# All three taps of w placed behind W's first mix and V's second level in VectorE's order

## The chip, the cores and the metric

The kernel runs on one core of a Trainium2 chip. The metric is the device time of one execution in microseconds (us), here the median of several runs. The five engines are TensorE (PE in the rows; PEld is its weight load), VectorE (DVE), ScalarE (ACT), GpSimd (POOL) and SyncE (SP). Each works through a queue of its own in order, and they wait for each other by semaphores.

## The reference, cut to what matters

A layer of gated slot attention over 4 sequences of 512 tokens with 16 heads of width 128, then a small feed-forward layer. Per head and sequence, h being the hidden states:

```python
q, k = short_conv(h @ Wq, cq), short_conv(h @ Wk, ck)
v, w = short_conv(h @ Wv, cv), short_conv(h @ Ww, cv)
g, beta = log_sigmoid(h @ Wf1 @ Wf2), sigmoid(h @ Wb)
w = l2norm(w)
# for each token t, with gt = exp(g_t) and bw = beta_t * w_t
Sk = Sk * gt + outer(k_t, bw)
Sv = Sv * gt + outer(bw, v_t)
a = softmax(q_t @ Sk * SCALE)
o_t = a @ Sv
```

short_conv is a causal filter of four taps over time for each channel, followed by silu. Its last tap (the present token) is a scaling; the other three are multiply-adds with the projection shifted by 1, 2 and 3 tokens. These three are "the taps" below.

## The kernel before

The recurrence over time is cut into levels of blocks of doubling length. 64 units (16 heads by 4 sequences) go through a pipeline: a slot is one pass of the loop over `slots(H, B)`, and in slot n unit n (`u1`) is projected and filtered, unit n-1 (`u2`) makes its scores level by level, unit n-2 (`u3`) takes them back level by level and makes the outputs, unit n-3 (`u4`) is normed and projected out, and unit n-4 (`u5`) is added up in memory. There are 68 slots; slots 2 to 63 hold all of u1, u2 and u3.

Every engine has its own copy of that loop, written out by hand. Nothing plans it: what stands earlier in an engine's body runs earlier, and each operation waits for the semaphores that it names.

What touches the change:

- `project(u, i)` on TensorE (lines 722 and 726 and on): six products into `proj_ps`, for w (i = 0), q (1), k (2), v (3). w and q use the same bank, `CONV_BANK = (0, 0, 1, 1)`.
- `tap` on ScalarE (line 347) scales the projection into `conv`. `conv_tap(dve, u, i, k)` on VectorE (line 591) adds the tap k = 0, 1, 2. The first waits for ScalarE's `tap_done`, the second and third for `conv_step` of the tap before. Each reads `proj_ps`.
- `tanh` on ScalarE (line 356) waits for the third tap. `silu_w` on VectorE (line 602) multiplies tanh and filter.
- On TensorE, `project(u1, 1)` for q stands at r = 1 of the slot and waits for `conv_step` of w's third tap, because it writes the bank that the taps read. Behind it come the projection of f (line 397) and the rest of the slot.
- `level_scores(pe, u2, r)` on TensorE (line 755 for r = 0 and 1, 777 from r = 2) makes the r-th level of V in `V_ps`, from the coarsest down. `descend(dve, u2, r)` on VectorE scales V between two levels: line 676 clears a part at r = 0, line 681 is r = 1, line 687 from r = 2. Each waits for the level before on TensorE, and the next level there waits for it.
- `mix_products(pe, u3, lev)` (line 806) and `mix_ends` (line 813) on TensorE, `mixable` (710) and `mix` (715, a masked copy) on VectorE and `grow_W` (298) on GpSimd take the scores back, from level 0 up. The masked copy of level 0 is "W's first mix". The third mix product on TensorE (level 2) is the first that waits for it, and stands behind `level_scores` of r = 1.

TensorE's order around the place is: `mix_ends`, mix product of level 1, key-query product, turn of U, `level_scores` r = 0, turn of U, `level_scores` r = 1, mix product of level 2, `project(u1, 1)`.

Of the kernel before, what the change touches and what calls it, by code (L numbers as in the profile page):

```python
# [61 lines left out]
def build(nc, x, Wq, Wk, Wv, Ww, cq, ck, cv, Wf1, Wf2, Wb, Wg1, Wg2, bg2, norm_w, Wo,  # L62
# [14 lines left out]
    with ExitStack() as ctx:  # L77
# [254 lines left out]
        def filt(u, i, k):  # L332

            return coefs[:, COEF_OF[i], u.h, k:k + 1]
# [251 lines left out]
        def conv_tap(dve, u, i, k):  # L586

            back = k + 1
            dve.wait_ge(tap_done, u.count(4, i + 1)) if k == 0 else dve.wait_ge(conv_step, u.count(12, 3 * i + k))
            y_ = conv[:, CONV_BUF[i], back:T]  # L590
            nc.vector.scalar_tensor_tensor(y_, proj_ps[:, CONV_BANK[i], 0:T - back], filt(u, i, KW - 1 - back), y_,  # L591
                                           ALU.mult, ALU.add).then_inc(conv_step, 1)
# [78 lines left out]
        def descend(dve, u2, r):  # L671

            lev = LEVELS - 1 - r
            if r == 0:
                wait(dve, V_done, u2.count(1, 0))
                nc.vector.memset(V_ps[:, 0:P], 0.0).then_inc(V_step, 1)
                return
            dve.wait_ge(V_ps_ready, u2.count(9, r))
            if r == 1:
                v = V_ps[:, 3 * P - 1:T]  # L680
                nc.vector.tensor_scalar(v, v, chunk_tot(u2.par, 2), None, ALU.mult).then_inc(V_step, 1)
                return
            if r == 2:
                v = V_ps[:, T - 1:T]
                nc.vector.tensor_scalar(v, v, chunk_tot(u2.par, 3), None, ALU.mult).then_inc(V_step, 1)
            v = after_odd(V_ps[:, :], lev)
            nc.vector.tensor_tensor(v, v, block_tot(u2.par, lev, 0), ALU.mult).then_inc(V_step, 1)  # L687
# [612 lines left out]
        def _(dve):  # L1300
# [7 lines left out]
            for s in slots(H, B):  # L1308
                u1, u2, u3, u4 = s.u1, s.u2, s.u3, s.u4
# [7 lines left out]
                if u2:  # L1317
# [1 line left out]
                    conv_tap(dve, u2, 3, 1)  # L1319
                    conv_tap(dve, u2, 3, 2)  # L1320
                    descend(dve, u2, 0)
                if u1:
                    conv_tap(dve, u1, 0, 0)
                    conv_tap(dve, u1, 0, 1)
                if u3:
                    mixable(dve, u3, 0)
                    mix(dve, 0)
# [2 lines left out]
                if u2:  # L1330
                    descend(dve, u2, 1)
                if u1:
                    conv_tap(dve, u1, 0, 2)
                for r in range(1, LEVELS):
                    if u2 and r > 1:
# [339 lines left out]
```

## Time and profile before

| | |
|---|---|
| median of 3 runs | 1989.41 us |
| lowest, highest | 1987.39, 1990.56 us |
| the profiled execution | 1987.3 us |
| its span, first to last instruction | 1985.6 us |
| granted TensorE clock, mean | 0.987 of full speed |
| busy: TensorE, VectorE | 97%, 89% of the span |
| busy: ScalarE, GpSimd | 70%, 67% |

The profile is of one execution. A busy time counts overlapping instructions once. Matmuls are pipelined and their ends are modelled, so their busy share is an upper look. The idle time of an engine before an instruction is shown in brackets with what ended it; idle times that are hidden under the end of the instruction ahead are not shown. A group of instructions in a timeline runs from the first start to the last end.

### The profile page before, as it was taken

To read this page: it belongs to the slowest core of one execution; us is meant where nothing else is said; L and a number is where in the kernel's file an instruction comes from. 1 tells how busy PE (TensorE), PEld (TensorE's weight loads), DVE (VectorE), ACT (ScalarE), POOL (GpSimd) and SP (SyncE) were. 2 spreads that over 40 slices of the span, in tenths; PEclk is the share of its full clock that TensorE was granted. 3 is DMA by queue.
4 is the path that set the end of the run, shared out by engine and by line. 5 is a ranking of instruction groups with operands and counts; after the bars stand their busy time and mean duration, and the time that the engine had idled before them with its cause. 6 is when DMAs were issued, how large, how long until landed. Compare 5 with 4: busy or idle time off the path is not lost.

```text
span 1985.6 us, 41492 instructions
## 1 busy us (share of the span) xinstructions
PE 1921.0 (97%) x12192; PEld 1623.8 (82%) x12192; DVE 1774.2 (89%) x4096; ACT 1395.3 (70%) x3986; POOL 1333.7 (67%) x2289
## 2 busy tenths in 40 slices
PE   7999999999999999999999999999999999999897
PEld 5778888888888888888888888888888888887776
DVE  5699999999999999999999999999999999998587
ACT  4467777777777777777777777777777777777543
POOL 5376676777677676767677676767677676766444
PEclk8899999999999999999999999999999999999899
DMA  3021111111111111111111110111111110112300
GB/s 78 1 61 21 27 34 24 26 24 33 26 24 27 27 34 20 30 24 33 27 24 26 27 35 15 36 24 33 23 27 26 24 37 14 25 22 43 63 22 33
DMA packets 53645, 58.51 MB, mean 29 GB/s; under 512 B 14896, under 2 KB 44720, under 8 KB 53424
## 3 DMA queue, kind: packets, MB, share of 16 engines
q0 software_dynamic: 9216, 33.56, 11.5%
q1 hardware_dynamic: 44208, 22.29, 4.1%
q8 instruction: 104, 1.70, 0.3%
q14 instruction: 117, 0.96, 0.2%
HBM read 20.19 MB, written 37.75 MB: 29 GB/s over the span
## 4 chain that ended last, share of the span: by engine, by line
PE 85%; POOL 7%; DVE 4%; issue 2%; ACT 1%; DMA 0%; POOLq 0%; DVEq 0%; ACTq 0%
PE proj_ps L722 15%; PE mix_ps L806 11%; PE V_ps L777 10%; PE work_ps L931 8%; PE work_ps L937 7%; PE tr_ps L746 6%; PE V_ps L755 5%; PE work_ps L1608 5%; PE proj_ps L397 4%; PE work_ps L826 3%; PE mix_ps L813 2%; POOL w_lo L370 2%; PE tr_ps L786 2%; PE work_ps L828 2%; PE proj_ps L1479 1%
## 5 line engine op out<-in xcount | busy, mean ns | idle before, releaser
L591 DVE SCALAR_TENSOR_TENSOR conv<-proj_ps,coefs,conv 128x511 f32<-128x511 f32 (+2 forms) x768 | 561.2, 731 | 9.9 <-ACT conv L347 3.0
L298 POOL TENSOR_TENSOR W<-W,tot 128x256 f32<-128x256 f32 x384 | 256.0, 667 | 245.3 <-PE mix_ps L806 245.1
L1059 POOL TENSOR_TENSOR A_lev<-A,masks 128x256 f32<-128x256 f32 x448 | 319.2, 717 | 0.1
L806 PE MATMUL mix_ps<-W,U 128*128 128x128 f32 x1792 | 294.6, 286 | 9.8 <-POOL W L298 4.3
L777 PE MATMUL V_ps<-A_lev,UT 128*128 128x128 f32 x1792 | 286.6, 283 | 1.4 <-DVE V_ps L687 1.4
L806 PEld LDWEIGHTS mix_ps<-W,U 128*128 128x128 f32 x1792 | 256.2, 192 | 35.7 <-issue 20.2
L715 DVE COPY_PREDICATED A<-masks,mix_ps 128x256 f32<-128x256 uint32 x448 | 268.5, 599 | 6.6 <-PE mix_ps L806 6.5
L584 DVE TENSOR_TENSOR wT<-wT,tot 128x128 f32<-128x128 f32 x768 | 233.2, 343 | 40.3 <-DVE U L567 1.8
L777 PEld LDWEIGHTS V_ps<-A_lev,UT 128*128 128x128 f32 x1792 | 238.0, 193 | 23.2 <-DVE V_ps L687 23.0
L356 ACT ACTIVATE th<-conv 128x512 f32<-128x512 f32 x256 | 162.3, 634 | 104.3 <-DVE conv L591 103.3
L722 PE MATMUL proj_ps<-hT_hi,w_hi 128*128 128x512 f32 x512 | 222.2, 434 | 4.2 <-DVE conv L591 2.4
L567 DVE COPY U<-wT 128x256 f32<-128x256 f32 x448 | 204.5, 457 | 7.2
L429 ACT ACTIVATE UT<-tr_ps 128x512 f32<-128x512 f32 (+1 forms) x256 | 139.1, 543 | 100.2 <-PE tr_ps L746 99.3
L687 DVE TENSOR_TENSOR V_ps<-V_ps,tot 128x256 f32<-128x256 f32 x384 | 163.8, 427 | 50.3 <-PE V_ps L777 50.2
L722 PE MATMUL proj_ps<-hT_hi,w_lo 128*128 128x512 f32 x512 | 203.0, 396 | 0.0
L722 PE MATMUL proj_ps<-hT_lo,w_hi 128*128 128x512 f32 x512 | 202.1, 395 | 0.0
L931 PE MATMUL work_ps<-qk 128*128 128x512 f32 (+3 forms) x512 | 182.2, 458 | 3.7 <-POOL qk L622 2.7
L298 POOL TENSOR_TENSOR W<-W,gT 128x256 f32<-128x256 f32 x64 | 54.2, 846 | 194.0 <-PE mix_ps L806 194.0
L347 ACT ACTIVATE conv<-proj_ps,coefs 128x512 f32<-128x512 f32 x256 | 175.4, 685 | 8.5 <-PE proj_ps L722 8.5
L414 ACT ACTIVATE A<-work_ps,fac 128x512 f32<-128x512 f32 (+3 forms) x256 | 128.0, 529 | 62.9 <-PE work_ps L931 62.6
L660 ACT ACTIVATE y_sb<-work_ps,rms 128x256 f32<-128x256 f32 x256 | 107.3, 471 | 55.0 <-PE work_ps L1608 54.9
L746 PE MATMUL tr_ps<-ident,U 128*128 128x128 f32 x896 | 140.1, 273 | 0.0
(204 smaller groups left out, 4763.2 us busy)
## 6 DMA issues: line engine op xcount, KB each, us to landing
head_sum<-y_sb POOLq DMA_DIRECT2D x64, 512.0 KB, 6.5
w_raw<-in_L_attn_Ww SPq DMA_DIRECT2D x16, 128.0 KB, 2.2
w_raw<-in_L_attn_Wq SPq DMA_DIRECT2D x16, 128.0 KB, 2.2
w_raw<-in_L_attn_Wk SPq DMA_DIRECT2D x16, 128.0 KB, 2.3
w_raw<-in_L_attn_Wv SPq DMA_DIRECT2D x16, 128.0 KB, 2.2
wo_raw<-in_L_attn_Wo SPq DMA_DIRECT2D x16, 128.0 KB, 2.0
head_sum<-in_L_attn_hidden_states SPq DMA_DIRECT2D x1, 2048.0 KB, 10.0
acc<-head_sum SPq DMA_DIRECT2D x4, 512.0 KB, 3.8
```

The lines of the kernel that those rows point to most:

```text
L298: nc.gpsimd.tensor_tensor(w, w, block_tot(u3.par, lev, 0), ALU.mult).then_inc(W_step, 1)
L347: nc.scalar.activation(conv[:, CONV_BUF[i], :], proj_ps[:, CONV_BANK[i], :], ACT.Copy, scale=filt(u, i, KW - 1)).then_inc(tap_done, 1)
L567: nc.vector.tensor_copy(Ulev(u, lev).rearrange("p (n e l) -> p n e l", e=2, l=L), merged(X, lev))\
L584: nc.vector.tensor_tensor(x_, x_, odd_tot(u.par, lev, e), ALU.mult).then_inc(U_step, 1)
L591: nc.vector.scalar_tensor_tensor(y_, proj_ps[:, CONV_BANK[i], 0:T - back], filt(u, i, KW - 1 - back), y_, ALU.mult, ALU.add).then_inc(conv ...
L715: nc.vector.copy_predicated(dst, mask_cols(lev).bitcast(U32), mix_cols(lev % 2, lev)).then_inc(mix_done, 1)
L722: last = nc.tensor.matmul(dst, w[:, k, :], x_(k), start=(k == 0 and n == 0), stop=(k == KT - 1 and n == 2))
L746: last = nc.tensor.transpose(tr_ps[:, n * P:(n + 1) * P], block_, ident[:, :])
L777: last = nc.tensor.matmul(dst, UT[:, i % 2, at:at + P], A_lev[:, lev, 2 * p:2 * p + 2, :], start=False, stop=True, skip_group_check=True)
L806: last = nc.tensor.matmul(mix_ps[:, half, p * P:(p + 1) * P], Ulev(u3, lev)[:, p * P:(p + 1) * P], after_odd(W[:, p * T // 2:(p + 1) * T / ...
L931: nc.tensor.matmul(work_ps[:, A_BANK[c], c * P:T], qk[:, 1, c * P:(c + 1) * P], qk[:, 0, c * P:T], start=True, stop=True).then_inc(A_ps_re ...
L1059: nc.gpsimd.tensor_tensor(dst, diag_after_odd(lev), mask_cols(lev), ALU.mult)\
```

## The change

VectorE's order at the beginning of a slot is changed, and nothing else. Before: v's three taps and the clearing of V (`descend` 0), w's first and second tap, W's first mix, V's second level (`descend` 1), w's third tap. After: v's three taps and the clearing, W's first mix, `descend` 1, all three taps of w. The instructions and what each of them waits for are the same.

```diff
@@ -1319,9 +1319,6 @@
                     conv_tap(dve, u2, 3, 1)
                     conv_tap(dve, u2, 3, 2)
                     descend(dve, u2, 0)
-                if u1:
-                    conv_tap(dve, u1, 0, 0)
-                    conv_tap(dve, u1, 0, 1)
                 if u3:
                     mixable(dve, u3, 0)
                     mix(dve, 0)
@@ -1330,6 +1327,8 @@
                 if u2:
                     descend(dve, u2, 1)
                 if u1:
+                    conv_tap(dve, u1, 0, 0)
+                    conv_tap(dve, u1, 0, 1)
                     conv_tap(dve, u1, 0, 2)
                 for r in range(1, LEVELS):
                     if u2 and r > 1:
```

## Rows read from the trace of the kernel before

**Rows 1.** The page: busy us, share of the span and instructions of each engine.

```profile
PE 1921.0 (97%) x12192; PEld 1623.8 (82%) x12192; DVE 1774.2 (89%) x4096; ACT 1395.3 (70%) x3986; POOL 1333.7 (67%) x2289
```

**Rows 2.** The page: the chain that ended last, by engine.

```profile
PE 85%; POOL 7%; DVE 4%; issue 2%; ACT 1%; DMA 0%; POOLq 0%; DVEq 0%; ACTq 0%
```

**Rows 3.** Window of four slots: length, busy PE, PEld, DVE, ACT, POOL, PEclk, DMA share, GB/s.

```profile
1018.00:1130.00 112.00, 110.82 (x717) 93.76 (x716) 103.93 (x241) 83.32 (x243) 78.94 (x139) 1.00 0.16 27
```

**Rows 4.** The chain in order of time, slot 35: start us, us, what.

```profile
1017.60 0.44 PE tr_ps L746 x4
...
1018.06 0.71 PE V_ps L755 x4
1018.77 0.53 PE mix_ps L806 x4
1019.30 1.39 PE proj_ps L722 x6
```

**Rows 5.** Timeline of VectorE, slot 35: start, us, engine, line, what, forms, count [idle].

```profile
1013.08 2.31 DVE L591 SCALAR_TENSOR_TENSOR conv<-proj_ps,coefs,conv 128x511 f32<-128x511 f32 x3
...
1015.49 1.46 DVE L591 SCALAR_TENSOR_TENSOR conv<-proj_ps,coefs,conv 128x511 f32<-128x511 f32 x2
...
1016.93 0.72 DVE L715 COPY_PREDICATED A<-masks,mix_ps 128x256 f32<-128x256 uint32 x1
1017.64 0.36 DVE L681 TENSOR_SCALAR V_ps<-V_ps,tot 128x129 f32<-128x129 f32 x1
1017.91 0.74 DVE L591 SCALAR_TENSOR_TENSOR conv<-proj_ps,coefs,conv 128x509 f32<-128x509 f32 x1
1018.57 0.75 DVE L611 SCALAR_TENSOR_TENSOR vT<-th,conv 128x256 f32<-128x256 f32 x2
```

**Rows 6.** Timeline of VectorE, slot 35, the second tap of w alone.

```profile
1016.20 0.75 DVE L591 SCALAR_TENSOR_TENSOR conv<-proj_ps,coefs,conv 128x510 f32<-128x510 f32 x1
```

**Rows 7.** Timeline of TensorE's weight loads, slot 35.

```profile
1018.05 0.52 PEld L755 LDWEIGHTS V_ps<-A,UT_top 128*128 128x128 f32 x4 [0.25 <-DVE V_ps L681]
...
1019.01 0.19 PEld L722 LDWEIGHTS proj_ps<-hT_hi,w_hi 128*128 128x128 f32 x1
```

**Rows 8.** Timelines of VectorE and TensorE at the place, slots 2, 7 and 63.

```profile
91.82 0.36 DVE L681 TENSOR_SCALAR V_ps<-V_ps,tot 128x129 f32<-128x129 f32 x1 [0.22 <-PE V_ps L755]
92.09 0.74 DVE L591 SCALAR_TENSOR_TENSOR conv<-proj_ps,coefs,conv 128x509 f32<-128x509 f32 x1
...
93.22 0.50 PE L722 MATMUL proj_ps<-hT_hi,w_hi 128*128 128x512 f32 x1
...
231.15 1.03 PE L755 MATMUL V_ps<-A,UT_top 128*128 128x257 f32 x4
...
232.40 0.39 DVE L681 TENSOR_SCALAR V_ps<-V_ps,tot 128x129 f32<-128x129 f32 x1
...
1803.34 0.74 DVE L591 SCALAR_TENSOR_TENSOR conv<-proj_ps,coefs,conv 128x509 f32<-128x509 f32 x1
...
1804.47 0.50 PE L722 MATMUL proj_ps<-hT_hi,w_hi 128*128 128x512 f32 x1
```

**Rows 9.** Timeline of ScalarE, slot 35: the tanh of w.

```profile
1018.74 0.63 ACT L356 ACTIVATE th<-conv 128x512 f32<-128x512 f32 x1 [1.48 <-DVE conv L591]
```

**Rows 10.** Timeline of VectorE, slot 35: V's next two steps behind the place.

```profile
1022.10 0.43 DVE L687 TENSOR_TENSOR V_ps<-V_ps,tot 128x256 f32<-128x256 f32 x1 [0.21 <-PE V_ps L777]
...
1023.89 0.43 DVE L687 TENSOR_TENSOR V_ps<-V_ps,tot 128x256 f32<-128x256 f32 x1 [0.20 <-PE V_ps L777]
```

**Rows 11.** Line 397 (ns min/median/max), a wait of TensorE, and two windows as in rows 3.

```profile
L397 PE MATMUL proj_ps<-f_hi,wf_hi x64: 393/394/628, 20.6 to 1806.0; 128*128 128x512 f32 x64
...
1836.59 0.57 PE L806 MATMUL mix_ps<-W,U 128*128 128x128 f32 x3 [1.25 <-POOL W L298]
...
1845.00:1850.00 5.00, 2.55 (x16) 1.54 (x14) 3.60 (x15) 3.27 (x11) 1.01 (x1) 0.96 0.02 5
1850.00:1855.00 5.00, 3.85 (x17) 3.49 (x16) 1.16 (x3) 4.90 (x11) 2.02 (x3) 0.50 0.21 15
```

## The prediction

> **What bounds the kernel now.** I read the busy shares first. TensorE is busy for 1921.0 of 1985.6 us, VectorE for 1774.2 [rows 1], and in a steady stretch of four slots TensorE records 110.82 of 112 us, VectorE 103.93 [rows 3]. The chain that ended last says the same by another way: 85% of it is TensorE's [rows 2]. So a slot is TensorE's queue in its order, and it comes round every 28.05 us: from 92.09 in slot 2 to 1803.34 in slot 63 for the same tap, over 61 slots [rows 8]. Recorded idle of TensorE is (112 - 110.82) / 4 = 0.30 us a slot, and that is all the slack that a wait could eat.
>
> Then I read one slot (slot 35) at the place of the change. In the chain in order of time, the first level's products of V end at 1017.60, TensorE turns U until 1018.04, V's second level runs from 1018.06 to 1018.77, a mix product to 1019.30, and from there the projection of q [rows 4]. On VectorE's side the second level's step of V (line 681) starts at 1017.64, 0.04 us behind the product that it waits for [rows 4, 5]. It has that same 0.04 us in 61 of 64 slots; slot 2 shows the wait with its name, 0.22 us on V_ps [rows 8]. Only slots 1, 7 and 56 have VectorE itself arriving last (slot 7: the product ends at 231.15 + 1.03 = 232.18, the step starts at 232.40 [rows 8]). So **VectorE meets TensorE at line 681 and is a little early there already**.
>
> The third tap of w follows it: start 1017.91, 0.74 us, end 1018.65 [rows 5]. TensorE's projection of q writes the bank that w's taps read, so it waits for that third tap. Its weight load starts at 1019.01, 0.36 us behind the tap's end [rows 7]. Between V's step and the projection the delay is fixed: in all 62 slots from 2 to 63 the projection's first product starts 1.13 us behind that tap's start (92.09 to 93.22, 1803.34 to 1804.47 [rows 8]).
>
> **The change part by part.**
>
> *Two taps leave the place ahead of the first mix.* They took 1.46 us there (from 1015.49) [rows 5]. The copy and the masked copy of the first mix come up to 1.4 us earlier; the far ends of the mix products, for which they wait, are ready at about the time at which the taps started. Who gains? V's step at line 681 doesn't: it waits for the product that ends at 1017.60, and nothing ahead of that product waits for a tap. The next user of the mix on TensorE stands behind V's second level in its own order, at 1018.77 [rows 4], over a microsecond behind the masked copy's end at 1017.65 [rows 5]. So this part is worth 0, and VectorE gets about 1.3 us more of idle time ahead of line 681 instead. The cover is that TensorE is last at line 681; in the three slots where it isn't, the gain is at most 0.2 to 0.5 us once, under 1 us in the run.
>
> *The two taps come in behind line 681.* All three now run in one chain, each waiting for the one before. The price of such a chain stands in the same slot: v's three taps take 2.31 us from start to end [rows 5]. Beginning 0.27 us behind V's step (1017.64 to 1017.91), they end 2.58 us behind it, where the one tap ended at 1.01. That is 1.57 us later. The other bound goes by w's own first two: the second starts at 1016.20, 0.71 us behind the first [rows 6], and not (2.31 - 0.74) / 2 = 0.79; with it for the first step the chain ends at 0.27 + 0.71 + 0.79 + 0.74 = 2.51, that is 1.50 us later.
>
> *TensorE waits for the third.* It had 0.36 us between the tap's end and the weight load. Of that a signal from VectorE needs some 0.05 us: V's step ends at 1018.00, the load that it releases starts at 1018.05 [rows 5, 7]. Slack is thus 0.31 us, and the stall is 1.50 - 0.31 = 1.19 to 1.57 - 0.31 = 1.26 us a slot. I take the middle, **1.22 us**. The projection of q and all behind it in TensorE's queue (f's projection, the levels of V, the turns, the mix products) move by that. Below nothing it can't go, since no instruction of TensorE between line 681 and the projection gets shorter.
>
> The Trainium skill, page "VectorE: DVE Perf Modes", section "The DRAIN you can't avoid", says that between VectorE operations a semaphore after each costs nothing over the flush that takes place anyway. The rows disagree: an operation that doesn't wait for the tap ahead starts 0.66 us behind its start (1017.91 to 1018.57 [rows 5]), a tap that waits 0.71 to 0.79 us. What the page's rule would give is the third rival below.
>
> *Who else is behind the taps?* VectorE's silu of v and V's next steps come 1.5 us later, 0.3 more than TensorE does. They were early: the masked copy after them let VectorE wait 0.21 and 0.20 us at V's next two steps [rows 10], which takes up 0.3 and brings VectorE back to TensorE's pace. On ScalarE the tanh of w waits for the third tap: it had waited 1.48 us [rows 9], and now waits 1.5 longer. The evacuation of U behind it moves by the same 1.5, and its reader on TensorE stands behind both projections, which take 1.39 us for q's six products alone [rows 4]. GpSimd has no operation that waits for a tap of w here, and no DMA or queue of SP is moved.
>
> **The sum.** Slots 2 to 63, 62 of them, pay 1.22 us: 75.6 us. Slot 0 has no V and no mix, so the order is the same; in slot 1 setup products lie between the tap and the projection and cover it; slot 64 and on have no w. The profiled execution took 1987.3 us (span 1985.6 and 1.7 around it), so it becomes 2062.9. The median of the runs shown lies 2.1 us above that execution, which gives 2065.0. I give **2064**, between both. In the profile I expect a slot of 29.27 us.
>
> **The rivals.**
>
> *Part of the stall is given back.* Waits of TensorE later in the slot for something that isn't late would shrink. All its recorded idle is 0.30 us a slot [rows 3], so at least 1.19 - 0.30 = 0.89 us a slot is left, and with it 55 us: 2043. Half of it gives 2054. Against it: most of these waits end on VectorE's or ScalarE's answer to a product of TensorE itself, and they move along.
>
> *VectorE's lag is not made up.* If it is the bound behind the taps, its whole 1.57 us goes round in each slot: 62 x 1.57 = 97 us, 2085. For it speaks its load (93% in the stretch [rows 3]), against it the two waits in [rows 10].
>
> *A cheaper chain.* If waiting taps followed each other like operations that don't wait, at 0.66 us, the third would end at 0.27 + 0.66 + 0.66 + 0.74 = 2.33 us behind V's step, 1.32 us later than now, and the stall would be 1.32 - 0.31 = 1.01 us: 63 us, 2051. The taps in [rows 5, 6] that already wait speak against it. (By the Trainium skill's section named above it would come out so.)
>
> *Clock.* Now TensorE would stand for over a microsecond in every slot. In this trace it stood 1.25 us until 1836.59, and the clock was still 0.96 from 1845 to 1850; it was 0.50 from 1850 to 1855, after a stretch in which TensorE was busy for only 2.55 of 5 us [rows 11]. Were each stall followed by the lower level (1.2 GHz) for the nine products of the two projections, each would take 0.63 in place of 0.39 us [rows 11]: 9 x 0.23 = 2.1 us a slot, 130 us more, 2194. [...] No steady slot of before shows a gap that long, so this is left to the run; I give it little, since 1.25 us did nothing.
>
> *Faster.* VectorE is the one that is late at line 681, as in slot 7. Then the step moves forward by all of that lateness, and V's second level with it. It decides from a lateness of 1.2 us, where it outweighs the stall; at the full 1.46 us of the two taps the gain is 0.24 us a slot, 15 us: 1972. The trace has 0.5 us at the most, in one slot.
>
> *It does nothing.* The projection would have to be released by something later than the taps. Then the time stays at 1989. The weight load follows so closely that 1.2 us more of cover isn't there.
>
> **How the numbers follow.** Chances: forecast (1.10 to 1.32 us a slot, 2057 to 2071) 0.60; part given back (2043 to 2057) 0.12; cheaper chain (about 2051) 0.03; VectorE's lag (2071 to 2085) 0.14; clock 0.04; more given back than recorded idle, 1995 to 2043, 0.03; no change 0.02; faster 0.02. A measurement of this kernel can tell about 0.2% from no change. The range takes in the first four and a few us beyond for the unknown costs: 2040 to 2087. Faster 0.02, same 0.02, slower 0.96.
>
> **What would show it.** Right: in VectorE's timeline the masked copy ends over a microsecond ahead of line 681 and a wait on V_ps stands before that; the three taps follow as one group of about 2.3 us; the weight load of the projection of q shows an idle time of about 1.2 us, released by the tap (line 591); the slot is 29.2 to 29.3 us. Wrong: line 681 moving forward against the end of the product before it; idle time of TensorE in the rest of the slot that shrinks (part given back) or grows at V's levels (VectorE's lag); a granted clock below 1.00 between 120 and 1850 us.

## The result

The changed kernel took 2067.86 us (median, 2067.6 to 2068.94), the kernel before 1989.99 us beside it: a ratio of 1.0394, 95% interval 1.0379 to 1.0408. That is 77.9 us slower; 2064 was forecast, from a sum of 75.6 us.

The page of the changed kernel, in the parts that answer to [rows 1, 2]: busy times and the chain that ended last by engine.

```profile
span 2067.2 us, 41492 instructions
...
PE 1941.5 (94%) x12192; PEld 1627.9 (79%) x12192; DVE 1777.6 (86%) x4096; ACT 1396.8 (68%) x3986; POOL 1326.4 (64%) x2289
...
PE 79%; DVE 10%; POOL 7%; issue 2%; ACT 1%; DMA 0%; POOLq 0%; DVEq 0%; ACTq 0%
```

VectorE's busy time is the same to 3.4 us, so it does no more work. Its share of the chain went from 4% to 10%: in each slot the chain now leaves TensorE for VectorE. The place shows in the chain in order of time, slot 35 of the changed kernel (start us, us, what), which answers to [rows 4].

```profile
1060.62 0.88 PE V_ps L755 x4
1061.51 0.02 issue
1061.53 0.36 DVE V_ps L681
1061.89 0.66 DVE conv L591
1062.55 0.02 issue
1062.58 0.76 DVE conv L591
1063.34 0.02 issue
1063.36 0.76 DVE conv L591
1064.12 0.04 issue
1064.16 1.65 PE proj_ps L722 x6
```

From the end of V's first level the chain runs through V's step and the three taps to the projection of q. Before, TensorE's own products filled that stretch. The timelines of VectorE and of TensorE's weight loads in the same slot answer to [rows 5, 7].

```profile
1059.31 0.17 DVE L676 MEMSET V_ps<- 128x128 f32 x1
1059.65 0.17 DVE L710 COPY A<-mix_ps 128x4 f32<-128x4 f32 x1 [0.18 <-PE mix_ps L813]
1059.73 0.73 DVE L715 COPY_PREDICATED A<-masks,mix_ps 128x256 f32<-128x256 uint32 x1
1061.53 0.36 DVE L681 TENSOR_SCALAR V_ps<-V_ps,tot 128x129 f32<-128x129 f32 x1 [1.08 <-PE V_ps L755]
1061.80 2.30 DVE L591 SCALAR_TENSOR_TENSOR conv<-proj_ps,coefs,conv 128x511 f32<-128x511 f32 x3
1064.02 1.25 DVE L611 SCALAR_TENSOR_TENSOR vT<-th,conv 128x256 f32<-128x256 f32 x2
```

```profile
1061.94 0.52 PEld L755 LDWEIGHTS V_ps<-A,UT_top 128*128 128x128 f32 x4 [0.25 <-DVE V_ps L681]
1062.39 0.57 PEld L806 LDWEIGHTS mix_ps<-W,U 128*128 128x128 f32 x4
1064.16 0.19 PEld L722 LDWEIGHTS proj_ps<-hT_hi,w_hi 128*128 128x128 f32 x1 [1.20 <-DVE conv L591]
```

The mix is over at 1060.46, and VectorE then idles 1.08 us until V's first level ends. The weight load of the projection starts 1064.16 - 1061.53 = 2.63 us behind line 681, where it was 1019.01 - 1017.64 = 1.37 [rows 5, 7]: **1.26 us later**, the upper of the two bounds. The slot is 29.30 us, from 94.77 in slot 2 to 1882.03 in slot 63 for the first tap behind line 681, over 61 slots; before it was 28.05 [rows 8].

### The profile page after: what moved, and what is told of

Same layout as the page of the kernel before. It is cut to its first block, busy times and chain, and to the rows that moved or that the text cites. A ratio compares the mean times of both kernels' runs of the same rounds, so it can differ in the third digit from the quotient of the medians.

```text
span 2067.2 us, 41492 instructions
## 1 busy us (share of the span) xinstructions
PE 1941.5 (94%) x12192; PEld 1627.9 (79%) x12192; DVE 1777.6 (86%) x4096; ACT 1396.8 (68%) x3986; POOL 1326.4 (64%) x2289
## 4 chain that ended last, share of the span: by engine, by line
PE 79%; DVE 10%; POOL 7%; issue 2%; ACT 1%; DMA 0%; POOLq 0%; DVEq 0%; ACTq 0%
PE proj_ps L722 16%; PE mix_ps L806 10%; PE V_ps L777 9%; PE work_ps L931 8%; DVE conv L591 7%; PE work_ps L937 7%; PE tr_ps L746 5%; PE work_ps L1607 5%; PE proj_ps L397 4%; PE V_ps L755 3%; PE work_ps L826 3%; PE mix_ps L813 2%; POOL w_lo L370 2%; PE tr_ps L786 2%; PE work_ps L828 2%
## 5 line engine op out<-in xcount | busy, mean ns | idle before, releaser
L591 DVE SCALAR_TENSOR_TENSOR conv<-proj_ps,coefs,conv 128x511 f32<-128x511 f32 (+2 forms) x768 | 566.8, 738 | 12.4 <-ACT conv L347 3.2
L1059 POOL TENSOR_TENSOR A_lev<-A,masks 128x256 f32<-128x256 f32 x448 | 309.1, 695 | 0.1
L777 PEld LDWEIGHTS V_ps<-A_lev,UT 128*128 128x128 f32 x1792 | 237.9, 192 | 23.5 <-DVE V_ps L687 23.3
L722 PEld LDWEIGHTS proj_ps<-hT_hi,w_hi 128*128 128x128 f32 x512 | 97.1, 190 | 103.5 <-DVE conv L591 76.9
```

Source lines behind the costliest of these rows:

```text
L722: last = nc.tensor.matmul(dst, w[:, k, :], x_(k), start=(k == 0 and n == 0), stop=(k == KT - 1 and n == 2))
L777: last = nc.tensor.matmul(dst, UT[:, i % 2, at:at + P], A_lev[:, lev, 2 * p:2 * p + 2, :], start=False, stop=True, skip_group_check=True)
L1059: nc.gpsimd.tensor_tensor(dst, diag_after_odd(lev), mask_cols(lev), ALU.mult)\
```

## The experiments

The theory: TensorE stands because w's third tap ends later behind line 681, and passing the mix is free. Rivals: the order against the mix costs (A); VectorE is the bound and its idle time is what is paid (B); the waits in themselves cost, whatever their length (C); a tap ahead of the mix is always free (D).

### Past the mix alone

```diff
                 if u1:
-                    conv_tap(dve, u1, 0, 0)
-                    conv_tap(dve, u1, 0, 1)
                 if u3:
                     mixable(dve, u3, 0)
                     mix(dve, 0)
+                if u1:
+                    conv_tap(dve, u1, 0, 0)
+                    conv_tap(dve, u1, 0, 1)
```

> The kernel before, with w's first two taps moved behind the first mix but still ahead of V's step at line 681; the third stays behind it. Theory (TensorE stalls for the taps that stand between line 681 and the projection of q; passing the mix is worth nothing): the third tap still ends about 1.0 us behind line 681, no stall. VectorE may wait some 0.18 us for the far ends ahead of the copy and reach line 681 that much later: 1990 to 2002 us, no stall of 1.2 us at the projection. Rival A (it is the order against the mix that costs): near 2068. Rival B (VectorE is the bound, and the 1.08 us that it idles ahead of line 681 in the changed kernel is what is paid): that idle time is filled again, so near 1990 too; this run doesn't tell B from the theory.

Measured: 1999.29 against 1990.27 us, ratio 1.0045 (1.0028 to 1.0062), 9 us. Its timeline of VectorE, slot 35:

```profile
1021.85 0.17 DVE L710 COPY A<-mix_ps 128x4 f32<-128x4 f32 x1 [0.17 <-PE mix_ps L813]
1021.93 0.73 DVE L715 COPY_PREDICATED A<-masks,mix_ps 128x256 f32<-128x256 uint32 x1
1022.45 1.50 DVE L591 SCALAR_TENSOR_TENSOR conv<-proj_ps,coefs,conv 128x511 f32<-128x511 f32 x2
1023.87 0.35 DVE L681 TENSOR_SCALAR V_ps<-V_ps,tot 128x129 f32<-128x129 f32 x1
```

Rival A is out. What the move past the mix costs is one idle time of 0.17 us ahead of the copy, whose far ends aren't ready so early; no wait stands before line 681 any more, so VectorE is last there. TensorE's weight load behind that line (1024.28) shows 0.38 us of idle time, where it had 0.25 [rows 7], and 9 us over 62 slots is 0.15 us each. Nearly all of the 78 us belongs to passing line 681.

### One tap moved

```diff
-                    conv_tap(dve, u1, 0, 1)
...
+                    conv_tap(dve, u1, 0, 1)
                     conv_tap(dve, u1, 0, 2)
```

> The kernel before, with only the second tap of w moved behind line 681 (one ahead of the mix, two in a chain behind). Theory: the third tap ends 0.27 + 0.78 + 0.75 = 1.80 us behind line 681, 0.79 later than before, less 0.31 of slack: a stall of 0.48 us in 62 slots, 30 us, 2020. Without any slack it would be 0.79 x 62 = 49 us, 2039; if half of the whole price is paid, 2029. Rival B (VectorE's idle time ahead of line 681 is what costs): about 0.4 to 0.5 us of idle time a slot, the same 25 to 31 us.

Measured: 2017.79 us, 27.5 us more than before (ratio 1.0140, 1.0124 to 1.0155). TensorE's weight load:

```profile
1034.62 0.19 PEld L722 LDWEIGHTS proj_ps<-hT_hi,w_hi 128*128 128x128 f32 x1 [0.42 <-DVE conv L591]
```

It starts 1.84 us behind line 681 (1032.78), 0.47 later than before; times 62 that is 29 us. One tap costs 28 us and two cost 78, not 56: the first pays only beyond the slack of 0.31 us, the second pays in full (1.26 - 0.47 = 0.79 us at the load, 49 us; the medians are 50 us apart). That is a threshold, as the sum had it, and not a price for each tap.

### The two taps cut short, at either place

```diff
-            y_ = conv[:, CONV_BUF[i], back:T]
-            nc.vector.scalar_tensor_tensor(y_, proj_ps[:, CONV_BANK[i], 0:T - back],
+            w_ = 8 if i == 0 and k < 2 and 1 < u.off else T - back
+            y_ = conv[:, CONV_BUF[i], back:back + w_]
+            nc.vector.scalar_tensor_tensor(y_, proj_ps[:, CONV_BANK[i], 0:w_],
```

> The kernel before with w's first two taps cut to 8 columns in slots 2 to 63 (part of the filter is left out; every wait and signal stays). VectorE loses about 1.2 us of work a slot ahead of the first mix. Theory (TensorE is last at line 681; what stands ahead of the mix is free): no gain beyond some 3 us, 1986 to 1991. Rival B (VectorE, busy 93% of a steady stretch, is the bound): its 1.2 us comes back in each slot, 74 us, 1916.

> The changed kernel with the same two taps cut to 8 columns (part of the filter is left out). Theory: the price is the length of the chain behind line 681; two short taps of 0.2 to 0.25 us with their waits bring the third tap's end to 1.4 to 1.6 us behind line 681, 0.4 to 0.6 later than before, less 0.31 of slack: 0.1 to 0.3 us a slot, 1996 to 2009. Rival C (the place and the waits in themselves cost, not the length): above 2040.

Measured: in the kernel before 1989.9 against 1990.51 us (ratio 0.9997, 0.9987 to 1.0007); in the changed kernel 2002.25 us (ratio to the kernel before 1.0057, 1.0042 to 1.0072). VectorE with the short taps in the kernel before, slot 35:

```profile
1019.38 0.42 DVE L592 SCALAR_TENSOR_TENSOR conv<-proj_ps,coefs,conv 128x8 f32<-128x8 f32 x2
1019.75 0.17 DVE L711 COPY A<-mix_ps 128x4 f32<-128x4 f32 x1
1019.83 0.72 DVE L716 COPY_PREDICATED A<-masks,mix_ps 128x256 f32<-128x256 uint32 x1
1021.53 0.36 DVE L682 TENSOR_SCALAR V_ps<-V_ps,tot 128x129 f32<-128x129 f32 x1 [0.98 <-PE V_ps L756]
```

The 1.46 us of [rows 5] became 0.42 us, and the 1.04 us of work that is gone turned into 0.98 us of idle time ahead of the step of V. Nothing came out at the end: rival B is out for this place in the kernel before. In the changed kernel the same cut gives back 66 of 78 us: the three taps take 1.26 us there in place of 2.30. So the length of the chain is what is paid, and rival C is out.

### The stall filled on TensorE

```diff
-        PROJ_AT = (1, 2, 4, 5)
+        PROJ_AT = (1, 3, 4, 5)
...
-                        pe.wait_ge(conv_step, u1.count(12, 3))
-                        pe.wait_ge(low_done, 4 * u1.h + 2)
-                        project(u1, 1)
                         pe.wait_ge(wf_low, u1.h + 1)
...
                         three_products(proj_ps[:, 1, :], wf_hi, wf_lo, ...)
+                        pe.wait_ge(conv_step, u1.count(12, 3))
+                        pe.wait_ge(low_done, 4 * u1.h + 2)
+                        project(u1, 1)
```

`PROJ_AT` tells ScalarE which of the projections of a unit it waits for; q's is the third now.

> The changed kernel, with TensorE's projection of f (the other bank, no wait for w's taps) moved ahead of the projection of q. VectorE's order and work are those of the changed kernel. Theory: f's three products (0.70 us) run inside the stall, q starts at the same 2.6 us behind line 681, the stall shrinks from 1.26 to 0.56 us: 62 x 0.70 = 43 us back, 2025. Rival B (VectorE is the bound): filling TensorE's wait gives nothing, 2060 to 2068. If the tap of q on ScalarE, 0.7 us later against the rest, becomes a new wait: between.

> The kernel before with the same exchange of f and q on TensorE, as the control of the run above. Theory: there is no stall to fill, q comes 0.7 us later and its readers have room: 1990, within 6. If q's lateness costs, it shows here: up to 0.7 x 62 = 43 us more, 2033.

Measured: 2042.3 us for the changed kernel with f first, 1992.11 us for the control (ratio 1.0011, 1.0002 to 1.0021). VectorE's order was left as it was and 25.6 us came back, which rules B out for the changed kernel too; but it isn't 43. What is missing stands in the waits of that run (waiting engine, tile and line, released by: us in total, times, longest), the second of which the kernel before and the changed one have once, for 0.4 us:

```profile
PEld proj_ps L722 <- DVE conv L591: 46.7, 63, 2.6
...
PEld V_ps L755 <- DVE V_ps L687: 25.9, 63, 0.6
```

With f no longer behind q, V's third level follows q's products at once, and meets V's step (line 687), which stands on VectorE behind the three taps and the silu of v. To test that, the silu of v was moved behind that step:

```diff
                     if u2 and r > 1:
                         descend(dve, u2, r)
-                    if u2 and r == 1:
-                        silu_v(dve, u2)
+                    if u2 and r == 2:
+                        silu_v(dve, u2)
```

> The changed kernel with f ahead of q on TensorE (2042 us) and, on VectorE, the silu of v moved behind V's next step. In the run without this move only 26 of the 43 us expected came back, and a new wait stood at V's third level (line 755, released by line 687, 25.9 us in 63 times). Theory: that wait is VectorE's lag behind the taps, laid open because f's products no longer cover it; without silu of v (1.25 us) ahead of that step it goes: 0.28 x 62 = 17 us back, 2025. If the lag isn't the cause, 2042. If v's turn on TensorE becomes late instead, between.

Measured: 2027.2 us (ratio to before 1.0178, 1.0159 to 1.0197), 15 us less, and the wait at line 755 on line 687 is down to 0.4 us, once. So VectorE's lag at that step of V is real, but in the changed kernel it lies under the projection of f.

### All three taps ahead

```diff
                     conv_tap(dve, u1, 0, 1)
+                    conv_tap(dve, u1, 0, 2)
...
-                if u1:
-                    conv_tap(dve, u1, 0, 2)
```

> The kernel before with all three taps of w ahead of the first mix, so none behind line 681. Theory: the copy and the masked copy come 0.75 us later, line 681 has 0.19 us in hand (it could start 0.52 us behind the masked copy's start and starts 0.71 behind), so V's second level and all of TensorE behind it move by about 0.55 us, while the wait for the tap at the projection is gone: 62 x 0.55 = 34 us, 2024. Rival D (a tap ahead of the mix is always free): 1990.

Measured: 2031.41 us (ratio 1.0201, 1.0186 to 1.0217), 41 us more; 34 were expected. The weight loads, slot 35:

```profile
1040.54 0.52 PEld L755 LDWEIGHTS V_ps<-A,UT_top 128*128 128x128 f32 x4 [0.91 <-DVE V_ps L681]
1040.98 0.57 PEld L806 LDWEIGHTS mix_ps<-W,U 128*128 128x128 f32 x4
1041.49 0.19 PEld L722 LDWEIGHTS proj_ps<-hT_hi,w_hi 128*128 128x128 f32 x1
```

Now the wait is V's: 0.91 us where it was 0.25 [rows 7], and none before the projection. 0.66 us times 62 is 41 us, so the 0.55 us expected were 0.11 too few. Rival D is out. Of the places tried for the three taps, the kernel before has the cheapest: two fit ahead of line 681, one behind it.

### The same kind of move where the step of V looks late

In the kernel before, TensorE waits 0.39 us for V's step of r = 7, and on VectorE k's first tap stands ahead of that step.

```diff
-                    if u1 and r in (6, 7):
-                        conv_tap(dve, u1, 2, r - 6)
+                    if u1 and r == 7:
+                        conv_tap(dve, u1, 2, 0)
+                        conv_tap(dve, u1, 2, 1)
```

> The kernel before with the same kind of move at another place, where the step of V may be what is late: the first tap of k goes behind V's step of r = 7 (line 687), for which TensorE's weight load waits 0.39 us. The reader of that chain of taps (the last tap of k, then tanh and the projection of v in the next slot) has over 2 us. Theory: V's step comes some 0.65 us earlier, TensorE's products before it end only 0.02 us before the level starts, so at most 0.1 to 0.15 us a slot comes back: 6 to 9 us, 1982. If the recorded 0.39 us were all real, 24 us, 1966. If the later taps of k are read sooner than that, slower: 2000.

Measured: 2024.97 us, 33 us more (ratio 1.0168, 1.0154 to 1.0182). The waits before and in this run at line 826, the outputs; the profile names no releaser there:

```profile
PEld work_ps L826 <- issue: 18.0, 62, 0.3
```

```profile
PEld work_ps L826 <- issue: 62.5, 63, 1.2
```

A miss of mine. The outputs wait for the masked copy of level 6, and both taps stand ahead of that copy, as they did before. What is new stands in VectorE's timeline of the run, slot 35:

```profile
1053.98 0.43 DVE L687 TENSOR_TENSOR V_ps<-V_ps,tot 128x256 f32<-128x256 f32 x1 [0.23 <-PE V_ps L777]
1054.33 0.48 DVE L715 COPY_PREDICATED A<-masks,mix_ps 128x256 f32<-128x256 uint32 x1
1054.68 1.51 DVE L591 SCALAR_TENSOR_TENSOR conv<-proj_ps,coefs,conv 128x511 f32<-128x511 f32 x2
```

The first tap used to run in the time ahead of V's step, where VectorE now waits 0.23 us, and the two taps now wait for each other. The copy ended at 1056.56, and the outputs' weights loaded from 1056.73. The gain at V's level was had, and more was lost one wait further on.

The run beside it had in addition the low part of k's weights behind the silu of k on GpSimd, in the slots ahead of a new head.

```diff
                     low_weights(pool, s.next_h, 1)
-                    low_weights(pool, s.next_h, 2)
...
                     silu_qk(pool, u1, 2)
+                if s.next_h:
+                    low_weights(pool, s.next_h, 2)
```

> The kernel of the run with k's tap behind V's step, and on GpSimd, in the slots ahead of a new head, the low part of k's weights (0.75 us) behind the silu of k instead of ahead of it. In these slots (one in four, 28.35 us against 27.86 to 28.02) the chain that ended last runs through GpSimd into the key-query products. Theory: these slots come down by 0.3 to 0.4 us, 15 x 0.35 = 5 us less than the run without it. If ScalarE's tanh of k, not GpSimd, is what the silu waits for, 0.

Measured: 2036.74 us, 12 us more than the run without it. The expectation was wrong in its sign. Only the slots ahead of a new head (one in four) became longer, 29.91 us against 28.90 in the median of twelve, from line 681 to line 681; and TensorE's weight loads at line 746 (turns of U) idled for 23.7 us in the run in place of 12.4, with no releaser named. Which reader of these weights or which step of GpSimd became late stays open.

With k's taps behind both masked copies:

```diff
                         mix(dve, 6)
+                    if u1 and r == 7:
+                        conv_tap(dve, u1, 2, 0)
...
                     if u1 and r == 8:
+                        conv_tap(dve, u1, 2, 1)
                         conv_tap(dve, u1, 2, 2)
```

> The kernel before with k's first tap behind V's step of r = 7 and behind the masked copies of levels 5 and 6, k's second tap behind V's step of r = 8, the third as before. In the earlier run (k's first and second tap both ahead of the masked copy of level 6) V's step came in time and TensorE saved some 0.16 us there, but the outputs (line 826) waited 1.00 us for that masked copy: 34 us slower. Theory: with no tap ahead of V's step or of the masked copy both waits go, 0.16 us at V's level and 0.25 us at the outputs; VectorE's work in the slot is the same, and at line 681 it has only 0.19 us in hand, so 0.2 to 0.4 us a slot: 1966 to 1979. If something behind reads k's taps sooner than it looks, slower than 1990.

Measured: 1994.34 us (ratio 1.0025, 1.0016 to 1.0034), a little slower than before. That is a sum of two signs: counted in the same way, a slot ahead of a new head took 28.89 us in place of 28.33, and the three behind it took 27.83, 27.78 and 27.78 us in place of 28.00, 28.00 and 27.84. Both waits went, and another took their place; this run's waits between 300 and 1700 us:

```profile
PEld work_ps L937 <- ACT aN L404: 39.1, 50, 2.0
...
ACT aN L404 <- DVE mx L544: 28.2, 50, 1.8
```

TensorE turns the scores' exponentials only when ScalarE has made them, ScalarE waits for their maximum, and that stands late in VectorE's order. In slot 35, which is ahead of a new head, the maximum even moved later. So it was moved up in all slots:

```diff
-                if u3 and not (u1 and u1.h and u1.par == 0):
-                    largest(dve, u3)
...
                     if u1 and r == 8:
                         grow_U(dve, u1, 2)
-                        copy_U(dve, u1, 3)
-                    if u2 and r == 8 and s.next_h:
+                    if u2 and r == 8:
                         largest(dve, u2)
                     if u1 and r == 8:
-                        scale_U(dve, u1, 3)
+                        grow_U(dve, u1, 3)
```

> The kernel of the run with k's taps behind the masked copy of level 6 (1994 us), and in every slot the maximum of the scores (line 544 before) moved ahead of the growing of U's level 3 on VectorE. In the run without this move TensorE and ScalarE reached the scores 0.6 us earlier in the slot, but VectorE took the maximum where its order had it, and the wait came back as TensorE's for the exponentials (39 us in 50 times); in the slots ahead of a new head that was 0.5 us later than before, and these slots alone made the run slower. Theory: with the maximum 0.2 us earlier (0.6 ahead of a new head) these waits shrink by as much, and VectorE's arrival at line 681 becomes the limit: 1975 to 1986, faster than the kernel before. If VectorE already sets the slot, or U's growth becomes late for its turn on TensorE: 1990 or more.

Measured: 2008.75 us (ratio 1.0095, 1.0078 to 1.0112). Between 300 and 1700 us:

```profile
PEld V_ps L755 <- DVE V_ps L681: 33.0, 49, 0.7
...
PE V_ps L755 <- DVE V_ps L681: 21.4, 49, 0.4
PEld tr_ps L746 <- ACT UT_top L429: 21.3, 49, 0.4
```

The wait for the exponentials fell to 3.6 us in 12 times, and line 681 is late now: TensorE itself stands there 21.4 us in 49 times, against 0.3 us once in the kernel before. VectorE had 0.19 us in hand there (the masked copy started at 1016.93 and line 681 0.71 us behind it [rows 5], where it can start 0.51 us behind, as the run with three taps ahead did). The likely reason is that the maximum ahead of the growing of U pushed the steps behind it; no run tests that. The slots ahead of a new head came down from 28.89 to 28.72 us, the others went up to 28.14 and 28.15. No version faster than the kernel before was found.

## Why the prediction was right

*The bound.* TensorE's order, with VectorE met at line 681: confirmed. Taking 1.04 us of VectorE's work away in front of it gave 0.6 us of 1990, less than can be told apart.

*The part worth nothing.* Two taps out from ahead of the mix: right for the changed kernel. The runs add what the text didn't have: passing the mix while staying ahead of line 681 costs 9 us, because the copy waits 0.17 us for the far ends. I had put them "at about the time" without that term. In the changed kernel it is hidden in the 1.08 us of idle time.

*The length of the chain.* I had two bounds, 1.50 and 1.57 us, and took the middle. The taps start at 1061.80, and the third ends at 1061.80 + 2.30 = 1064.10 by the timeline (1064.12 in the chain), 2.57 to 2.59 us behind line 681 against 1.01: the bound of v's chain (2.31 us in [rows 5]) was right and w's own short first step (0.71 us) wasn't. Behind the clearing at line 676 w's first tap took 0.67 us (1030.63 in the run with one tap moved), behind line 681 it took 0.74; why, no run shows. The term was 1.22 us and measured 1.26 us at the load, 1.25 us in the slot.

*The slack.* 0.31 us, held by the run with one tap: 0.79 - 0.47 = 0.32 us.

*The sum.* 61 slots of 1.25 us are 76 us between slot 2 and slot 63, and slot 63 adds its own; forecast 75.6, medians apart by 77.9. The two profiled executions lie 81.6 us apart; the rest of that is filling and draining the pipeline, where the clock changes from run to run (granted 0.82 from 20 to 48 us before, 0.77 in the changed kernel).

*Part given back.* It didn't happen in the changed kernel: the waits of TensorE on line 687 are 23.3 us at line 777 against 23.0, the one at line 755 on line 681 is 16.0 against 16.6 us. They move along with what releases them.

*VectorE's lag.* It cost nothing, but not for the reason given. The waits at V's next two steps were to take up 0.3 us a slot; the waits of line 687 on TensorE only fell from 50.2 to 47.0 us in the whole run, 0.05 us a slot. What took the lag up is the silu of w. First the kernel before, then the changed one, slot 35:

```profile
1019.70 1.55 DVE L602 SCALAR_TENSOR_TENSOR wT<-th,conv 128x256 f32<-128x256 f32 x2
...
1021.16 0.72 DVE L715 COPY_PREDICATED A<-masks,mix_ps 128x256 f32<-128x256 uint32 x1
```

```profile
1065.66 0.74 DVE L602 SCALAR_TENSOR_TENSOR wT<-th,conv 128x256 f32<-128x256 f32 x2
1066.33 0.72 DVE L715 COPY_PREDICATED A<-masks,mix_ps 128x256 f32<-128x256 uint32 x1
```

The silu of w starts 4.13 us behind line 681 in place of 2.06, 0.8 us more than TensorE's delay. The masked copy behind it starts 4.80 us behind line 681 in place of 3.52, and these 1.28 us are TensorE's delay again. The silu of v takes 0.50 us longer and that of w 0.81 us less; over the run both together keep VectorE busy for 128.5 us in place of 145.4, 0.27 us a slot. No such term is in the prediction, so that this rival failed was in part luck. The last section has what the runs show of the two silus. Until the silu of w is over the lag was covered by the projection of f, 0.70 us between q and V's third level, which I hadn't named either; with f ahead of q the gain fell short of the expected 43 us by 17 us, 0.28 us a slot.

*A cheaper chain.* Waiting taps follow each other by 0.78 us (1061.80, 1062.58, 1063.36), not by 0.66. The tap ahead of an operation that doesn't wait for it is followed after 0.66 us, also at 1063.36 to 1064.02. The Trainium skill, page "VectorE: DVE Perf Modes", section "The DRAIN you can't avoid", has from copies that a semaphore after each costs nothing; for these taps the measurement decides against it, by 0.12 us a tap. The same section says, too, that a next operation that isn't held starts earlier, and the 0.66 us agree with that.

*Clock.* The stall of 1.2 us in every slot left it at 1.00. In the changed kernel (windows, columns as in rows 3):

```profile
120.00:1800.00 1680.00, 1606.34 (x10259) 1344.51 (x10260) 1489.12 (x3437) 1194.52 (x3484) 1128.69 (x1979) 1.00 0.15 26
```

TensorE was busy for 1606 of these 1680 us. The Trainium skill, page "TensorE: Matmul & The Clock Gate", section "HAM oscillation — how this bites in real kernels", tells of a kernel whose clock fell again and again, with waits of 3 to 5 us for a DMA in each round; the shorter stalls here didn't do that. The rival's price was a little high, too: with the granted clock at 0.50 (36 to 40 us, kernel before) such products start 0.43 us apart, in slot 35 0.23 us, so that nine would cost 9 x 0.20 = 1.8 us a slot and not 2.1.

## What to carry to other kernels

Where two engines meet at a step in their orders, ask for each piece of work which side of that step it stands on and how much slack its own reader has: ahead of the step it is free up to the engine's time in hand, behind it up to the reader's slack, and beyond that each slot pays in full. Price a chain of dependent instructions by the same chain elsewhere in the trace, in the same surroundings, and not by its shortest link. Before moving work behind one awaited step, list all the awaited steps that it then still stands ahead of, and ask what the engine will do in the place that it leaves: three of my own moves failed on the next awaited step. When a change moves one engine against another, look whether operations that weren't touched got longer or shorter.

## What the runs showed of the hardware that I had not expected

The silu of v and that of w (two operations each, two operands from SBUF) exchanged their times in the changed kernel, with no change to either. First the kernel before, then the changed one (ns min/median/max):

```profile
L611 DVE SCALAR_TENSOR_TENSOR vT<-th,conv x128: 410/417/644, 48.6 to 1831.7; 128x256 f32<-128x256 f32 x128
...
L602 DVE SCALAR_TENSOR_TENSOR wT<-th,conv x128: 362/753/882, 19.8 to 1805.8; 128x256 f32<-128x256 f32 x128
```

```profile
L611 DVE SCALAR_TENSOR_TENSOR vT<-th,conv x128: 410/612/928, 51.3 to 1911.6; 128x256 f32<-128x256 f32 x128
...
L602 DVE SCALAR_TENSOR_TENSOR wT<-th,conv x128: 361/408/882, 19.9 to 1886.2; 128x256 f32<-128x256 f32 x128
```

What differs is GpSimd beside them. In the kernel before and then in the changed one, slot 35:

```profile
1019.45 0.71 POOL L298 TENSOR_TENSOR W<-W,tot 128x256 f32<-128x256 f32 x1 [1.18 <-PE mix_ps L806]
...
1020.11 0.85 POOL L1059 TENSOR_TENSOR A_lev<-A,masks 128x256 f32<-128x256 f32 x1
```

```profile
1063.34 0.70 POOL L298 TENSOR_TENSOR W<-W,tot 128x256 f32<-128x256 f32 x1 [1.18 <-PE mix_ps L806]
1064.00 0.67 POOL L1059 TENSOR_TENSOR A_lev<-A,masks 128x256 f32<-128x256 f32 x1
```

The silu of v (1064.02 to 1065.27) meets GpSimd's masking of A, and the silu of w behind it (from 1065.66) meets none of its large operations. Before, it was the other way round: the silu of v ended at 1019.32, and that of w ran from 1019.70 to 1021.25. In the two traces all 186 silu operations of v and w that took over 0.70 us lay beside an operation of GpSimd of over 0.5 us, and of the 320 that took under 0.43 us five did for more than 0.2 us. An operation of this kind, with both operands in SBUF, thus takes 0.41 us alone and mostly 0.75 to 0.92 us beside GpSimd, while the taps, which read PSUM too, keep their 0.65 to 0.75 us. The coincidence in time is shown; what the two engines share was not tried, and no run held GpSimd back to test it.
